# The relation loop's weights of a unit loaded by one transfer instead of six

## The chip, the cores and the metric

The kernel runs on one core of a Trainium2 chip. The metric is the device time of a whole execution in microseconds; of several runs the median is given.

## The reference

A graph with 625 nodes and 10,625 edges goes through four layers, each of which adds its output to the rows x [625, 768] after a layer norm and relu. Everything is float32. The first layer is the one at issue; for each of 34 relations r it takes the mean of the source rows over the edges of that relation at each target node, multiplies by the relation's 768 x 768 matrix, and adds all relations up:

```python
seg = edge_type * n + dst
agg = jax.ops.segment_sum(x[src], seg, num_segments=N_REL * n)
cnt = jax.ops.segment_sum(ones, seg, num_segments=N_REL * n)
mean = agg.reshape(N_REL, n, -1) / jnp.maximum(cnt, 1.0).reshape(N_REL, n, 1)
h1 = jnp.einsum('rni,rio->no', mean, W_rel) + x @ W_root + b_rgcn
```

The rest of the first layer is a graph convolution on h1; after it come two graph convolutions, three relational layers with 3 relations, and one more graph convolution.

## The kernel before

The program sorts the edges twice (by relation and source tile for the later layers, by relation alone for the first), plans the first layer's work, runs the relation loop `add_means` (L1415), and then the other layers.

The plan cuts the sorted edges into units. A unit has up to 3 x 128 edges of one relation and two or three tiles of 128 target slots. For each unit the loop does this:

- POOL gathers the 3 x 128 source rows by indirect DMA (`gather`, L1536) into e_raw, [128, 3, 768].
- SyncE loads the unit's list of targets (L1507) and the relation's weights (L1512) into w_raw, [128, 6, 768]: six chunks of 128 input features, each 384 KB. In `load(u)` chunk f waits until VectorE has split chunk f of the unit before, since w_raw has one buffer; every chunk has a semaphore `w_loaded[f]`.
- Products are made of two float32r parts. ScalarE casts each e tile and each weight chunk to a high part (`split_e` L1594, `split_w` L1598), VectorE subtracts it from the raw values for the low part (L1647, L1652). The parts w_hi, w_lo, e_hi, e_lo have one buffer each.
- TensorE first forms the unit's sums (L1718): rows of e times a 0/1 matrix `pick` that VectorE makes from the list (L1641), 36 matmuls. ScalarE and VectorE copy them out as g_hi and g_lo (L1614, L1670). Then come the products (L1732) of g with w, 36 matmuls for each target tile.
- ScalarE and VectorE scale the result into y (L1627, L1680), and POOL adds y to the sums in memory by an indirect DMA (`scatter`, L1548).

The order on each engine is written out by hand; all run a loop over the units. ScalarE and VectorE split chunk 5 of unit u inside the unit, right after the first bank of sums. During the products of unit u they split, for unit u+1, in the order w0, w1, e0, w2, e1, w3, e2, w4; ScalarE's w_f waits until the products have used chunk f of unit u (`w_used`). Then both scale y. TensorE's sums of u+1 wait for all e_lo of u+1. POOL in its turn u waits for e_ready of unit u, gathers for u+1, waits for the scatters of u-1 and issues the scatters of u when y is there. Transfers of SyncE are in one queue, those of POOL in another.

Of the kernel before, what the change touches and what calls it, by code (L numbers as in the profile page):

```python
# [55 lines left out]
def semaphores(nc, tag, ctx):  # L56


    made = []

    def clear():
        nc.clear_and_free_semaphores(made)
        nc.all_engine_barrier()

    ctx.callback(clear)

    def sem(name):
        made.append(nc.alloc_semaphore(f"{tag}_{name}"))
        return made[-1]

    return sem
# [1343 lines left out]
def add_means(nc, tag, units, w_rel, rows, sums, plan, src_index, slot_dst, row_index, row_inv, targets):  # L1415
# [8 lines left out]
    fc = width // 128  # L1424
    half = width // 2
    with ExitStack() as ctx:
        def sb(name, shape, dt):
            return ctx.enter_context(nc.sbuf_tensor(f"{tag}_{name}", shape, dt))

        sem = semaphores(nc, tag, ctx)  # L1430
# [9 lines left out]
        w_raw = sb("w_raw", [128, fc, width], F32)  # L1440
# [4 lines left out]
        ps_y = ctx.enter_context(nc.psum_tensor(f"{tag}_ps_y", [SLOT, UNIT, 2, BANK], F32))  # L1445

        list_loaded = sem("list_loaded")
        w_loaded = [sem(f"w_loaded{f}") for f in range(fc)]
        index_ready = sem("index_ready")
        gathered = [sem(f"gathered{j}") for j in range(UNIT)]  # L1450
        scattered = [sem(f"scattered{j}") for j in range(UNIT)]
# [4 lines left out]
        w_ready = sem("w_ready")  # L1456
# [8 lines left out]
        def count(eng):  # L1465

            return eng.value_load(plan[0:1, 3, 0:1], min_val=1, max_val=units - 1)

        def unit(u):
            return nc.s_assert_within(u, 0, units - 2, skip_runtime_bounds_check_because="units - 1 bounds their number")  # L1470

        def has_third(eng, u):
            return eng.value_load(plan[0:1, 1, bass.ds(u, 1)], min_val=0, max_val=1)

        def if_third(eng, third, body):

            with eng.If(third):
                body(3)
            with eng.Else():
                body(2)  # L1480

        def per_bank(tiles):

            return BANK // (tiles * SLOT)

        def sums_in_bank(i, tiles):

            per = per_bank(tiles)
            bank = ps_y[:, 2, i - 2, :] if is_spare(i) else ps_g[:, i % 2, :]
            return bank[:, 0:per * tiles * SLOT].rearrange("p (c s) -> p c s", c=per)  # L1490
# [9 lines left out]
        @block.sync  # L1500
        def _(sp):
            def load(u, first):
                kind = sp.value_load(plan[0:1, 0, bass.ds(u, 1)], min_val=0, max_val=w_rel.shape[0] - 1)
                if not first:

                    sp.wait_ge(picked, u)
                sp.dma_start(list_now[:], targets[bass.ds(u, 1), :].broadcast_to([SLOT, UNIT_COLS])).then_inc(list_loaded, 16)  # L1507
                for f in range(fc):
                    if not first:

                        sp.wait_ge(w_ready, fc * u - fc + f + 1)
                    sp.dma_start(w_raw[:, f, :], w_rel[bass.ds(kind, 1), f * 128:(f + 1) * 128, :].rearrange("a f o -> f (a o)"))\  # L1512
                        .then_inc(w_loaded[f], 16)

            load(0, True)
            end = count(sp)
            with sp.Fori(1, end + 1) as u:
                load(nc.s_assert_within(u, 1, units - 1, skip_runtime_bounds_check_because="as above"), False)

            sp.wait_ge(w_loaded[fc - 1], 16 * end + 16)  # L1520
            sp.sem_inc(waited, 1)

        @block.gpsimd
# [64 lines left out]
        @block.scalar  # L1588
        def _(act):
            nc.scalar.preload_act_table(ACT.Copy)  # L1590

            def split_e(u, j):
                act.wait_ge(gathered[j], 16 * u + 16)
                nc.scalar.copy(e_hi[:, j, :], e_raw[:, j, :]).then_inc(e_hi_ready, 1)  # L1594

            def split_w(u, f):
                act.wait_ge(w_loaded[f], 16 * u + 16)
                nc.scalar.copy(w_hi[:, f, :], w_raw[:, f, :]).then_inc(w_hi_ready, 1)  # L1598

            for j in range(UNIT):  # L1600
                split_e(0, j)
            for f in range(fc - 1):
                split_w(0, f)

            nc.scalar.nop().then_inc(y_ready, 2)
            with act.Fori(0, count(act)) as n:
                u = unit(n)
                third = has_third(act, u)

                def split_g(tiles):  # L1610
                    per = per_bank(tiles)
                    for f in range(0, fc, per):
                        act.wait_ge(g_summed, fc * u + f + per)
                        nc.scalar.copy(g_hi[:, f:f + per, 0:tiles * SLOT], sums_in_bank(f // per, tiles)).then_inc(g_hi_ready, per)  # L1614
                        if f == 0:

                            split_w(u, fc - 1)

                if_third(act, third, split_g)

                for f in range(fc):

                    act.wait_ge(w_used, fc * u + f + 1)
                    if f == fc - 1:

                        act.wait_ge(y_free, u + 1)
                        nc.scalar.activation(y[:, 1, :].rearrange("p (a o) -> p a o", a=2), ps_y[:, 1, :, 0:half], ACT.Copy,  # L1627
                                             scale=row_inv[:, bass.ds(UNIT * u + 1, 1)]).then_inc(y_ready, 1)
                    else:
                        split_w(u + 1, f)  # L1630
                    if 0 < f <= UNIT:
                        split_e(u + 1, f - 1)
# [107 lines left out]
def gnn_kernel(nc, d, out):  # L1740
# [11 lines left out]
    with ExitStack() as ctx:  # L1752
# [17 lines left out]
        with ExitStack() as part:  # L1770
            def sb(name, shape, dt):
                return part.enter_context(nc.sbuf_tensor(name, shape, dt))

            slot_src = sb("s0_slot_src", [SLOT, UNIT * units], F32)
            slot_dst = sb("s0_slot_dst", [SLOT, UNIT * units], F32)
            src_index = sb("s0_src_index", [SLOT, UNIT * units], I32)
            row_index = sb("s0_row_index", [SLOT, UNIT * units], I32)
            row_inv = sb("s0_row_inv", [SLOT, UNIT * units], F32)
            plan = sb("s0_plan", [1, 4, units], I32)
            with ExitStack() as early:  # L1780
                lots = early.enter_context(nc.sbuf_tensor("s0_lots", [EP, types0], F32))
                tile_of = early.enter_context(nc.sbuf_tensor("s0_tile_of", [EP, EC], F32))
                sort_edges(nc, "s0_sort", d["src"], d["dst"], d["edge_type_34"], types0, UNIT, slot_src, slot_dst,
                           lots=lots, tile_of=tile_of,
                           aside=lambda where, block, sem: root_rows(nc, where, block, sem, h, d["L0_gnn_b_rgcn"],
                                                                     d["L0_gnn_W_root"], ident, rows0, sums0[0:N, :]))
                plan_units(nc, "s0_plan", d["dst"], types0, tile_of, lots, slot_src, slot_dst, units, src_index,
                           row_index, row_inv, targets, plan, dinv)
            add_means(nc, "l0_means", units, d["L0_gnn_W_rel"], rows0, sums0, plan, src_index, slot_dst, row_index,
                      row_inv, targets)  # L1790
# [56 lines left out]
```

## Time and profile before

| | |
|---|---|
| median of 3 runs | 2092.66 us (2090.81 to 2101.08) |
| profiled execution, first to last instruction | 2085.4 us |
| TensorE matmul busy | 1726.6 us (83%) |
| VectorE busy | 1171.2 us (56%) |
| ScalarE busy | 592.7 us (28%) |
| POOL busy | 327.8 us (16%) |
| mean granted TensorE clock | 0.906 |
| DMA | 230.03 MB, mean 110 GB/s |

Of the profiled execution no other time than its span is given, so the runs' median stands beside the span. Busy shares are means over stages. The relation loop lies between about 365 and 1140 us of the span. Rows name a line of the kernel, the engine, the operation and output<-inputs; "waited for" rows say which engine's work ended an idle time. PE is TensorE, DVE VectorE, ACT ScalarE, SP SyncE; the suffix q is an engine's sequencer, which issues its transfers. The granted clock is a share of full speed.

### The profile page before, as it was taken

The page shows a single profiled execution, that of the slowest core. Times are in us where ns is not written, and L with a number is a line of the kernel's source. Part 1 is how long each engine was busy: PE and PEld are TensorE (multiplying, and loading weights), DVE is VectorE, ACT ScalarE, POOL GpSimd, SP SyncE. Part 2 cuts the span into 40 slices and gives each one's busy share as a digit, 9 for nine tenths or more (in the row PEclk, how much of TensorE's full clock was granted, in tenths as well). Part 3 has the DMA queues.
Part 4 walks back from the last instruction along what each step waited for, and adds up shares of the span by engine and source line. Part 5 has one row for each costly group of instructions (what it writes and reads, how often), then busy time and mean ns, then how long its engine had stood idle before and what let it go on. Part 6 is the DMA issues. An engine that isn't in the chain of part 4 may idle for free. (4 is left out here: it accounts for less than half of the span.)

```text
span 2085.4 us, 30218 instructions
## 1 busy us (share of the span) xinstructions
PE 1726.6 (83%) x10272; PEld 1655.3 (79%) x10273; DVE 1171.2 (56%) x1803; ACT 592.7 (28%) x782; POOL 327.8 (16%) x301
## 2 busy tenths in 40 slices
PE   2633954779889788889897599899998999999988
PEld 2532834779889788889896599799998999999988
DVE  8678697556566555565564464733554433444463
ACT  0112100444454443354443322211222211222221
POOL 1005010333434343323333000000000000000000
PEclk9675975899999999999998699899999999999999
DMA  1012100676877777678666311221222111122211
GB/s 62 4 43 87 39 1 2 209 230 196 219 216 200 226 209 200 170 230 226 194 199 157 109 37 58 66 54 65 77 65 60 57 52 45 52 72 65 60 46 53
DMA packets 84461, 230.03 MB, mean 110 GB/s; under 512 B 10326, under 2 KB 22617, under 8 KB 84410
## 3 DMA queue, kind: packets, MB, share of 16 engines
q1 hardware_dynamic: 65066, 158.14, 23.5%
q0 software_dynamic: 19344, 71.18, 14.6%
q8 instruction: 35, 0.57, 0.1%
q14 instruction: 16, 0.13, 0.0%
HBM read 190.01 MB, written 39.28 MB: 110 GB/s over the span
## 5 line engine op out<-in xcount | busy, mean ns | idle before, releaser
L1062 PE MATMUL layers_ps_o<-layers_w_hi,layers_g_hi 128*125 128x384 f32 (+1 forms) x1040 | 362.5, 349 | 4.1 <-DVE layers_w_lo L926 2.9
L1063 PE MATMUL layers_ps_o<-layers_w_lo,layers_g_hi 128*125 128x384 f32 (+1 forms) x1040 | 361.1, 347 | 0.0
L1064 PE MATMUL layers_ps_o<-layers_w_hi,layers_g_lo 128*125 128x384 f32 (+1 forms) x1040 | 360.4, 347 | 0.0
L1652 DVE TENSOR_TENSOR l_means_w_lo<-l_means_w_raw,l_means_w_hi 128x768 fp32r<-128x768 f32 x209 | 199.3, 955 | 97.3 <-ACT l_means_w_hi L1598 85.6
L1087 PE MATMUL layers_ps_g<-a,h_hi 125*128 125x316 f32 x840 | 197.2, 317 | 52.9 <-DVE h_lo L554 40.0
L1732 PE MATMUL l_means_ps_y<-l_means_w_hi,l_means_g_hi 128*128 128x384 f32 x912 | 231.5, 334 | 0.0
L1732 PE MATMUL l_means_ps_y<-l_means_w_hi,l_means_g_lo 128*128 128x384 f32 x912 | 231.5, 334 | 0.0
L1732 PE MATMUL l_means_ps_y<-l_means_w_lo,l_means_g_hi 128*128 128x384 f32 x912 | 231.4, 334 | 0.0
L1718 PE MATMUL l_means_ps_g<-l_means_pick,l_means_e_hi 128*128 128x256 f32 (+1 forms) x408 | 131.4, 342 | 102.3 <-DVE l_means_e_lo L1647 102.3
L1598 ACT CAST l_means_w_hi<-l_means_w_raw 128x768 fp32r<-128x768 f32 x209 | 173.7, 833 | 136.7 <-PE l_means_ps_y L1732 120.5
L1062 PEld LDWEIGHTS layers_ps_o<-layers_w_hi,layers_g_hi 128*125 128x125 f32 x1040 | 194.1, 187 | 13.9 <-DVE layers_g_lo L931 4.3
L1548 POOL DMA_INDIRECT sums<-l_means_y,l_means_row_now x76 | 142.2, 1871 | 398.7 <-DVE l_means_y L1680 374.3
L1064 PEld LDWEIGHTS layers_ps_o<-layers_w_hi,layers_g_lo 128*125 128x125 f32 x1040 | 194.0, 187 | 5.5
L1063 PEld LDWEIGHTS layers_ps_o<-layers_w_lo,layers_g_hi 128*125 128x125 f32 x1040 | 193.9, 186 | 5.3
L1087 PE MATMUL layers_ps_g<-a,h_lo 125*128 125x316 f32 x840 | 195.3, 315 | 0.0
L1087 PEld LDWEIGHTS layers_ps_g<-a,h_hi 125*128 125x128 f32 x840 | 144.2, 195 | 57.6 <-DVE h_lo L554 41.5
L1647 DVE TENSOR_TENSOR l_means_e_lo<-l_means_e_raw,l_means_e_hi 128x768 fp32r<-128x768 f32 x105 | 100.2, 955 | 150.9 <-ACT l_means_e_hi L1594 150.6
L1718 PEld LDWEIGHTS l_means_ps_g<-l_means_pick,l_means_e_hi 128*128 128x128 f32 x408 | 93.7, 230 | 110.6 <-issue 110.6
L942 DVE SCALAR_TENSOR_TENSOR h_rows<-layers_ps_o,h_rows 125x768 f32<-125x768 f32 (+1 forms) x45 | 45.1, 1002 | 237.9 <-PE layers_ps_o L1064 237.9
L1732 PEld LDWEIGHTS l_means_ps_y<-l_means_w_hi,l_means_g_lo 128*128 128x128 f32 x912 | 164.7, 188 | 0.0
L1732 PEld LDWEIGHTS l_means_ps_y<-l_means_w_lo,l_means_g_hi 128*128 128x128 f32 x912 | 164.6, 188 | 0.0
L1732 PEld LDWEIGHTS l_means_ps_y<-l_means_w_hi,l_means_g_hi 128*128 128x128 f32 x912 | 163.4, 188 | 0.0
(281 smaller groups left out, 2572.3 us busy)
## 6 DMA issues: line engine op xcount, KB each, us to landing
l_means_w_raw<-in_L_gnn_W_rel SPq DMA_DIRECT2D x210, 384.0 KB
layers_w_raw<-in_L_gnn_w_rel SPq DMA_DIRECT2D x39, 384.0 KB, 3.3
layers_w_raw<-in_L_gnn_w_rel SPq DMA_DIRECT2D x21, 448.0 KB, 3.7
layers_a_raw<-adj SPq DMA_DIRECT2D x9, 769.0 KB
layers_w_raw<-in_L_gnn_W SPq DMA_DIRECT2D x18, 384.0 KB, 5.2
l_means_list_now<-targets SPq DMA_DIRECT2D x35, 192.0 KB
layers_w_raw<-in_L_gnn_w_root SPq DMA_DIRECT2D x13, 384.0 KB, 3.6
layers_w_raw<-in_L_gnn_w_root SPq DMA_DIRECT2D x7, 448.0 KB, 4.1
```

The costliest lines, as they stand in the source:

```text
L942: v.scalar_tensor_tensor(to, ps, by, base, ALU.mult, ALU.add).then_inc(o_taken, 1)
L1062: t.matmul(out, g_hi[:, f, rows], w_hi[:, f, cols], start=(f == 0), stop=False)
L1063: t.matmul(out, g_hi[:, f, rows], w_lo[:, f, cols], start=False, stop=False)
L1064: mm = t.matmul(out, g_lo[:, f, rows], w_hi[:, f, cols], start=False, stop=(f == fc - 1))
L1087: mm = t.matmul(ps_g[:, buf, at:at + PART[p]], rows[:, k, f * 128:(f + 1) * 128], a[:, k, cols], start=(k == 0 and part == 0), stop=(k == ...
L1548: nc.gpsimd.indirect_dma_start(out=sums, in_=y[:, j, :], in_offset=None, compute_op=ALU.add, out_offset=bass.IndirectOffsetOnAxis(ap=row_n ...
L1598: nc.scalar.copy(w_hi[:, f, :], w_raw[:, f, :]).then_inc(w_hi_ready, 1)
L1647: v.tensor_tensor(e_lo[:, j, :], e_raw[:, j, :], e_hi[:, j, :].bitcast(F32), ALU.subtract)\
L1652: v.tensor_tensor(w_lo[:, f, :], w_raw[:, f, :], w_hi[:, f, :].bitcast(F32), ALU.subtract)\
L1718: mm = t.matmul(sums, e[:, j, f * 128:(f + 1) * 128], pick[:, j, 0:cols], start=(j == 0 and part == 0), stop=(j == UNIT - 1 and part == 1))
L1732: mm = t.matmul(ps_y[:, j, o, 0:half], g[:, f, at], w[:, f, o * half:(o + 1) * half], start=(f == 0 and g is g_hi and w is w_hi), stop=(f ...
```

## The change

In the relation loop, the six weight transfers of a unit and their six semaphores become one transfer and one semaphore. The transfer waits until all six chunks of the unit before are split (`w_ready` at 6u). ScalarE's split of any chunk waits for the whole transfer. The list's transfer before it, the order of the splits and all else are unchanged.

```diff
@@ -1445,7 +1445,7 @@
-        w_loaded = [sem(f"w_loaded{f}") for f in range(fc)]
+        w_loaded = sem("w_loaded")
@@ -1505,19 +1505,18 @@
-                for f in range(fc):
-                    if not first:
-
-                        sp.wait_ge(w_ready, fc * u - fc + f + 1)
-                    sp.dma_start(w_raw[:, f, :], w_rel[bass.ds(kind, 1), f * 128:(f + 1) * 128, :].rearrange("a f o -> f (a o)"))\
-                        .then_inc(w_loaded[f], 16)
+                if not first:
+
+                    sp.wait_ge(w_ready, fc * u)
+                sp.dma_start(w_raw[:], w_rel[bass.ds(kind, 1), :, :].rearrange("a (f p) o -> p (a f) o", p=128))\
+                    .then_inc(w_loaded, 16)
...
-            sp.wait_ge(w_loaded[fc - 1], 16 * end + 16)
+            sp.wait_ge(w_loaded, 16 * end + 16)
@@ -1594,7 +1593,7 @@
             def split_w(u, f):
-                act.wait_ge(w_loaded[f], 16 * u + 16)
+                act.wait_ge(w_loaded, 16 * u + 16)
                 nc.scalar.copy(w_hi[:, f, :], w_raw[:, f, :]).then_inc(w_hi_ready, 1)
```

## Rows read from the trace of the kernel before

**Rows 1.** Window of the loop: us, engines' busy, PEclk, DMA share, GB/s.
```profile
377.80:1136.60 758.80, 669.13 (x3960) 660.63 (x3960) 435.38 (x579) 338.40 (x470) 270.85 (x244) 0.94 0.74 206
```

**Rows 2.** The page's costliest groups, one kind of product.
```profile
L1732 PE MATMUL l_means_ps_y<-l_means_w_hi,l_means_g_hi 128*128 128x384 f32 x912 | 231.5, 334 | 0.0
```

**Rows 3.** Waits of TensorE in the whole profile: total us, times, longest.
```profile
PE l_means_ps_g L1718 <- DVE l_means_e_lo L1647: 102.3, 26, 17.7
```

**Rows 4.** Windows, summed, of the 19 two-tile units after a two-tile unit.
```profile
sum 382.20, PE 344.53 PEld 338.55 DVE 232.18 ACT 180.55 POOL 139.48; mean PE 18.13 PEld 17.82 DVE 12.22 ACT 9.50 POOL 7.34
```

**Rows 5.** Windows, summed, of six two-tile units after a three-tile unit.
```profile
sum 148.60, PE 101.77 PEld 99.86 DVE 74.66 ACT 62.18 POOL 59.49; mean PE 16.96 PEld 16.64 DVE 12.44 ACT 10.36 POOL 9.91
```

**Rows 6.** Windows of the six three-tile units after a two-tile unit, two of them.
```profile
639.60:664.60 25.00, 25.00 (x144) 25.00 (x145) 14.24 (x20) 10.69 (x16) 8.16 (x7) 1.00 0.68 191
...
821.00:848.80 27.80, 27.78 (x145) 27.79 (x146) 14.40 (x20) 10.00 (x15) 6.56 (x7) 0.90 0.63 177
```

**Rows 7.** Timeline of VectorE in one unit: start, us, instruction, idle before.
```profile
712.11 0.96 DVE L1652 TENSOR_TENSOR l_means_w_lo<-l_means_w_raw,l_means_w_hi 128x768 fp32r<-128x768 f32 x1
...
718.62 0.96 DVE L1652 TENSOR_TENSOR l_means_w_lo<-l_means_w_raw,l_means_w_hi 128x768 fp32r<-128x768 f32 x1 [1.03 <-ACT l_means_w_hi L1598]
724.56 0.96 DVE L1647 TENSOR_TENSOR l_means_e_lo<-l_means_e_raw,l_means_e_hi 128x768 fp32r<-128x768 f32 x1 [4.98 <-ACT l_means_e_hi L1594]
...
728.10 0.95 DVE L1647 TENSOR_TENSOR l_means_e_lo<-l_means_e_raw,l_means_e_hi 128x768 fp32r<-128x768 f32 x1
```

**Rows 8.** Timeline of ScalarE in the same unit.
```profile
723.69 0.84 ACT L1594 CAST l_means_e_hi<-l_means_e_raw 128x768 fp32r<-128x768 f32 x1 [5.11 <-DMA l_means_e_raw<-rows,l_means_src_now]
...
726.96 0.83 ACT L1594 CAST l_means_e_hi<-l_means_e_raw 128x768 fp32r<-128x768 f32 x1
```

**Rows 9.** Timeline of TensorE, the first matmul of the next unit.
```profile
729.18 0.38 PE L1718 MATMUL l_means_ps_g<-l_means_pick,l_means_e_hi 128*128 128x256 f32 x1 [3.14 <-DVE l_means_e_lo L1647]
```

**Rows 10.** Timeline of SyncE's issues, 705 to 735.
```profile
706.40 7.17 SPq L1512 DMA_DIRECT2D l_means_w_raw<-in_L_gnn_W_rel  x4
...
717.75 16.02 SPq L1512 DMA_DIRECT2D l_means_w_raw<-in_L_gnn_W_rel  x6
```

**Rows 11.** Waits of ScalarE before the weight casts.
```profile
ACT l_means_w_hi L1598 <- PE l_means_ps_y L1732: 120.5, 77, 2.7
```

**Rows 12.** Lines L1512 and L159: issues, ns min/median/max, first and last start.
```profile
L1512 SPq DMA_DIRECT2D l_means_w_raw<-in_L_gnn_W_rel x210: 332/333/567, 365.5 to 1118.8; - x105
...
L159 SPq DMA_DIRECT2D sums<-s_sort_spare x1: 443/443/443, 7.8 to 7.8; - x1
```

**Rows 13.** Waits of SyncE before the weight issues.
```profile
SPq L1512 <- DVE l_means_w_lo L1652: 505.5, 200, 11.7
```

**Rows 14.** Timeline of VectorE ahead of the sums at 539.53.
```profile
534.97 0.96 DVE L1647 TENSOR_TENSOR l_means_e_lo<-l_means_e_raw,l_means_e_hi 128x768 fp32r<-128x768 f32 x1 [9.68 <-ACT l_means_e_hi L1594]
...
539.32 0.95 DVE L1652 TENSOR_TENSOR l_means_w_lo<-l_means_w_raw,l_means_w_hi 128x768 fp32r<-128x768 f32 x1
```

**Rows 15.** Timeline of TensorE, the sums at 539.53.
```profile
539.53 0.57 PE L1718 MATMUL l_means_ps_g<-l_means_pick,l_means_e_hi 128*128 128x256 f32 x1 [7.78 <-DVE l_means_e_lo L1647]
```

**Rows 16.** Windows for the DMA engines (last two columns: share, GB/s).
```profile
713.00:727.00 14.00, 13.04 (x77) 12.72 (x75) 6.70 (x11) 5.35 (x8) 5.83 (x7) 1.00 0.88 239
...
375.00:377.00 2.00, 0.00 (x0) 0.00 (x0) 1.28 (x2) 1.29 (x3) 0.00 (x0) 0.50 1.00 389
```

**Rows 17.** Timeline of POOL, the first gather of the unit at 709.
```profile
716.23 1.04 POOL L1536 DMA_INDIRECT l_means_e_raw<-rows,l_means_src_now  x1 [0.84 <-POOL l_means_src_now L1533]
```

**Rows 18.** The page's DMA issues, a later layer's weights: KB each, us to landing.
```profile
layers_w_raw<-in_L_gnn_w_rel SPq DMA_DIRECT2D x39, 384.0 KB, 3.3
```

**Rows 19.** Windows of the sums of two units, granted clock third from the end.
```profile
539.50:545.70 6.20, 6.17 (x37) 6.17 (x38) 3.82 (x5) 1.91 (x3) 3.21 (x2) 0.67 0.67 159
...
559.10:563.40 4.30, 4.30 (x36) 4.30 (x37) 3.50 (x5) 2.21 (x4) 1.63 (x1) 1.00 0.63 183
```

## The prediction

> **What bounds the kernel now.** I read the loop first, then its units, then one unit engine by engine. The relation loop takes 758.8 us of the profiled execution [rows 1]. It has 34 units: the 912 matmuls of each product kind are 76 tiles of 12, so 26 units of two tiles and 8 of three [rows 2] (in the windows below, 108 or 144 matmuls). TensorE's longest waits in the whole profile stand there, 26 of them, all for e_lo, the last input that a unit's sums need [rows 3]. So the loop is not bound by TensorE in two-tile units. The order of units, read off the starts of the sums, gives classes: 19 two-tile units after a two-tile one, 20.1 us each with 18.1 busy [rows 4]; 7 two-tile units after a three-tile one, 24.8 us each in the six that are followed by another, with 17.0 busy [rows 5]; 6 three-tile units after a two-tile one, busy throughout, 25.0 or 25.1 us and, once, 27.8 [rows 6]; and two more three-tile units, the first and the last but one.
>
> One unit in detail, its sums starting at 709.0; I call that S. VectorE splits the unit's own last chunk (w5) at S+3.1 to S+4.1, makes the pick, then splits w0 and w1 of the next unit, w1 at S+9.6, and stands idle 4.98 us until the first gathered tile is there [rows 7]. ScalarE's own wait in front is for the gather [rows 8]. From S+15.6 six passes e0, w2, e1, w3, e2, w4 follow each other, e2 ends at S+20.1, and the next sums start at S+20.2 [rows 7, 9]. The point for this change is that no weight is waited for: SyncE sends each chunk as soon as its old content is split [rows 10], so chunks 0 to 4 of the next unit are sent up to a whole unit ahead, and only w5 is sent within the unit itself. ScalarE's waits before w_hi are for the products that free w_hi, 120.5 us in 77 waits, and none is for a weight transfer [rows 11].
>
> **What the change removes.** Five issues per unit on SyncE, 0.33 us each [rows 12]. SyncE is no bound: it waits for VectorE 505.5 us at that line [rows 13]. Gain taken: nothing. Its cover is that wait, and if it were gone, 5 x 0.33 = 1.7 us a unit would be the most. A single three-piece transfer from 128 partitions took 0.44 us to issue [rows 12], so the new issue is priced at 0.4 us. The loop's list transfer is still sent ahead of the weights and waits for the same pick: no change, and the pick is made before the next list is needed.
>
> **What it adds: a wait.** The one transfer may start only when all six chunks of the unit before are split, that is after its w5, S+4.1. And the first split of the next unit needs all six to have landed. Transfer and splitting, which went on side by side, now stand one behind the other. The sequence is w5 split, transfer T, then w0, w1, e0, w2, e1, w3, e2 on VectorE, then the sums.
>
> *The tail behind the landing.* In the unit before 539.53 the passes from e0 to w4 ran without a gap at 0.87 us each, from 534.97, and the sums started 4.56 us after e0 started [rows 14, 15]. Two more passes (w0, w1) make 4.56 + 2 x 0.87 = 6.3, and ScalarE's cast ahead of the first makes 0.9 [rows 8]: the next sums start 7.2 us after the landing. Behind the waiting cast ScalarE also has the casts of e, so an e that is there earlier does not help.
>
> *The transfer.* It is 6 x 128 x 3 KiB = 2.36 MB. From 713 to 727 the DMA engines moved 239 GB/s x 14 us = 3.35 MB at a share of 0.88 [rows 16]. That is just the unit's traffic: two scattered tiles 0.79, three gathered 1.18, the list 0.20, and three weight chunks (w5, w0, w1) 1.18. The other three chunks went in the quieter end. Now all six are asked for in this stretch: 1.18 MB more. With weights nearly alone the engines did 389 GB/s at share 1.00 [rows 16], so 3.0 us more. Against that stands the unused 12% of 14 us, 1.7 us, which a waiting transfer can fill. The stretch ends at 728.3 to 730.0, S+19.3 to S+21.0; the gather shares the engines from S+7.2 [rows 17] and the weights finish last but for the list behind them (0.5 us). Landing: S+18.8 to S+20.5. I take S+19.3, near the lower end, because a queue that always has weight packets fills the gaps. Lower bound of all: a 384 KB chunk in the later layers lands in 3.3 us [rows 18], of which 1.0 is its data at 389 GB/s, so the six on idle engines would land 2.3 + 6.1 = 8.4 us after the issue, S+12.9.
>
> *The clock.* TensorE would idle from about S+17 to S+26.5. After an idle of 7.8 us the next sums ran at a mean granted clock of 0.67 and took 6.2 us, where at clock 1.00 they took 4.3 [rows 15, 19]; the levels are 1.2 and 2.4 GHz. This puts the w5 split at S+5.3 instead of S+4.1; scatter occupies the engines then in any case, and S+19.3 has that start in it.
>
> **The sum.** Two-tile after two-tile: period 19.3 + 7.2 = 26.5 against 20.1, +6.4, times 19 = 122 us. Two-tile after three-tile: three scatters keep the gather late already, so the weights (sent at S+4.0, first sums fast) land by about S+18 and the tail would end at S+25.2; what binds is still the gather, delayed by the extra weight traffic, between 0 and 3.0 us. I take 1.5, times 7 = 10 us. Three-tile units: products cover the transfer (S+19.3 + 7.2 is before 27.8), but their sums now come after an idle TensorE, as in the one of 27.8 us: +2.7 for five of the six [rows 6], 13 us. First unit: its products wait until all six chunks have landed, 1 us. Sum +146 us. The profiled execution is given by its span, 2085.4, which becomes 2231; the median of the three runs shown, 2092.66, stands 7.3 above it, so 2239 us.
>
> **A page against this.** The trace has no large weight transfer to time. The Trainium skill, DMA: Bandwidth & Descriptors, Rules for kernel authors, wants at least 1 MiB per DMA on 128 partitions, and its section Anatomy of one DMA gives about 2.0 us plus bytes / 436 GB/s (for the gpsimd path); an estimate from it is 7.4 us for this one. The same table also says to issue early and wait late, which is what is lost here. By its formula alone the landing would be at S+12.7, the rival next.
>
> **Rivals.**
> A. *The weights get through first.* For it: with 2.36 MB asked for at once they may take more than their share, and the idle-engine bound is S+12.9. The gather then ends 3.0 us later than now (its last cast starts at S+18.0 [rows 8]), at S+20.9, and with the 2.2 us from there to the next sums the period is 23.1: +3.0 x 19, +3.0 x 7, +13 = 91 us, 2184. Against it: scatter and gather are queued over the same stretch, which is already at 0.88. This is also where the formula of the Trainium skill's DMA page leads.
> B. *The clock stays up,* as in the unit at 559.1. Then w5 is split 1.2 us earlier, the landing is about S+18, the period 25.2, three-tile units stay at 25.1: 19 x 5.1 + 10 = 107, 2200.
> C. *Weights starve.* Scatter and gather hold the engines, landing at S+21.3, 28.5 a period: 19 x 8.4 + 7 x 3.5 + 14 = 198, 2291.
> D. *Hidden, no change:* needs landing by S+12.9 and a gather no later. Excluded by the share 0.88 unless the scatter's share is mostly idle waiting.
> E. *Faster.* Place: the gather. If the burst is over before the gather's first packet, w0 and w1 (0.79 MB, 2.0 us) no longer share the engines with it, and the period falls from 20.1 to 18.1: 19 x 2 = -38, 2055. It decides only if the burst lands by S+10, under 6 us after its issue, less than its data take at 389 GB/s.
>
> **Chances.** Forecast 0.65, A 0.10, B 0.12, C 0.08, D 0.03, E 0.02. The range runs from A to just short of C, 2180 to 2285; it holds the bounds of the landing (S+18.8 and S+20.5 are 19 x -0.5 and 19 x +1.2, so 2229 and 2262) and B. A measurement here tells about 0.5%, 10 us, from no change. Faster 0.02, same 0.03, slower 0.95.
>
> **What would show it.** One weight issue a unit, about S+4 to S+5.4, and none within the products. ScalarE's first w_hi of the next unit waits for the weight transfer, and then seven casts follow without a gap. TensorE's waits for e_lo stay about 26 in number but grow to 8 to 10 us each. Two-tile units of 25 to 28 us with granted clock under 1.00 at the sums, three-tile units of 27.8. The stages before 365 and after 1150 unchanged. I am wrong if the landing is before S+15, if the seven casts still wait for the gather, or if two-tile periods stay near 20.

## The result and the profile after

The changed kernel takes 2261.19 us (median of 4 runs, 2259.78 to 2264.04) against 2091.73 of the kernel before in the same series: a ratio of 1.079 [1.077, 1.082], 169.5 us slower. Forecast were 2239 us, +146, with a range of 2180 to 2285. The profiled execution took 2264.04 us as a whole and 2262.0 from first to last instruction, so only 2 us lie around the span. The spans differ by 176.6 us, 7 more than the medians: before's profiled execution lay some 4 us below its median, and the changed kernel's is the longest of its four, 2.9 us above.

The windows of the units, grouped as in [rows 4 to 6]: the 19 two-tile units after a two-tile one, the six after a three-tile one, and the six three-tile units (columns as there: TensorE, its weight loads, VectorE, ScalarE, POOL).

```profile
sum 537.60, PE 363.27 PEld 357.29 DVE 228.21 ACT 175.78 POOL 136.81; mean PE 19.12 PEld 18.80 DVE 12.01 ACT 9.25 POOL 7.20
...
sum 153.30, PE 102.24 PEld 100.35 DVE 76.34 ACT 60.70 POOL 55.08; mean PE 17.04 PEld 16.72 DVE 12.72 ACT 10.12 POOL 9.18
...
sum 164.70, PE 163.52 PEld 162.72 DVE 80.38 ACT 58.39 POOL 39.63; mean PE 27.25 PEld 27.12 DVE 13.40 ACT 9.73 POOL 6.61
```

| units | before, us | forecast | after | share of the loss |
|---|---|---|---|---|
| 19 two-tile after two-tile | 20.1 | 26.5 | 28.3 | 19 x 8.2 = 155.4 |
| 7 two-tile after three-tile | 24.8 | 26.3 | 25.6 (six) | 7 x 0.8 = 5.5 |
| 6 three-tile after two-tile | 25.5 | 27.7 | 27.5 | 6 x 1.9 = 11.5 |

The three, taken from the unrounded sums, make 172 of the spans' 176.6 us. In the first class VectorE and ScalarE do what they did; what grew is idle time. Waits in the loop of the changed kernel, most time first, others left out at the dots:

```profile
ACT l_means_w_hi L1597 <- DMA l_means_w_raw<-in_L_gnn_W_rel: 428.6, 34, 15.1
DVE l_means_w_lo L1651 <- ACT l_means_w_hi L1597: 409.5, 41, 14.2
...
PE l_means_ps_g L1717 <- DVE l_means_e_lo L1646: 245.4, 28, 18.8
...
ACT l_means_w_hi L1597 <- PE l_means_ps_y L1731: 12.0, 1, 12.0
ACT l_means_e_hi L1593 <- DMA l_means_e_raw<-rows,l_means_src_now: 11.6, 8, 8.1
```

Before, ScalarE waited for no weights at all, only for the products that free w_hi [rows 11]; that wait has all but gone, and 34 waits for the weights stand in its place. The wait for the gather, 156 us in the loop before, is down to 11.6: the gathered tiles are there, but their casts stand behind one that waits. TensorE's wait went from 102 us in 26 [rows 3] to 245 in 28.

One two-tile unit whose sums start at S = 623.0. First ScalarE, then VectorE, SyncE and TensorE (start, us, instruction, idle before and what ended it):

```profile
629.91 0.59 ACT L1613 CAST l_means_g_hi<-l_means_ps_y 128x512 fp32r<-128x512 f32 x1 [0.85 <-PE l_means_ps_y L1717]
643.91 1.56 ACT L1597 CAST l_means_w_hi<-l_means_w_raw 128x768 fp32r<-128x768 f32 x2 [13.41 <-DMA l_means_w_raw<-in_L_gnn_W_rel]
645.38 0.83 ACT L1593 CAST l_means_e_hi<-l_means_e_raw 128x768 fp32r<-128x768 f32 x1
...
648.31 0.83 ACT L1593 CAST l_means_e_hi<-l_means_e_raw 128x768 fp32r<-128x768 f32 x1
```
```profile
627.41 0.96 DVE L1651 TENSOR_TENSOR l_means_w_lo<-l_means_w_raw,l_means_w_hi 128x768 fp32r<-128x768 f32 x1
...
644.77 1.83 DVE L1651 TENSOR_TENSOR l_means_w_lo<-l_means_w_raw,l_means_w_hi 128x768 fp32r<-128x768 f32 x2 [12.37 <-ACT l_means_w_hi L1597]
...
649.99 0.95 DVE L1646 TENSOR_TENSOR l_means_e_lo<-l_means_e_raw,l_means_e_hi 128x768 fp32r<-128x768 f32 x1
```
```profile
628.54 0.38 SPq L1511 DMA_DIRECT2D l_means_w_raw<-in_L_gnn_W_rel  x1
```
```profile
651.07 0.58 PE L1717 MATMUL l_means_ps_g<-l_means_pick,l_means_e_hi 128*128 128x256 f32 x1 [8.77 <-DVE l_means_e_lo L1646]
```

w5 is split by S+5.4, the transfer goes out at S+5.5 (0.38 us to issue), the first cast starts at S+20.9, seven casts follow without a gap, the last e part is ready at S+27.9 and the sums start at S+28.1. From the cast to the sums are 7.16 us; 7.2 was forecast. TensorE idles 8.77 us before the next sums. This unit's own sums, which came after such an idle too, ran at a granted clock of 0.61 and took 6.6 us:

```profile
623.00:629.60 6.60, 6.55 (x36) 6.56 (x37) 3.76 (x5) 1.90 (x3) 3.59 (x3) 0.61 0.28 30
```

### The profile page after: what moved, and what is told of

Same layout as the page of the kernel before. It is cut to its first block and busy times, and to the rows that moved or that the text cites. A ratio compares the mean times of both kernels' runs of the same rounds, so it can differ in the third digit from the quotient of the medians.

```text
span 2262.0 us, 29557 instructions
## 1 busy us (share of the span) xinstructions
PE 1756.1 (78%) x10272; PEld 1683.5 (74%) x10273; DVE 1162.0 (51%) x1803; ACT 581.1 (26%) x782; POOL 310.9 (14%) x301
## 5 line engine op out<-in xcount | busy, mean ns | idle before, releaser
L1717 PE MATMUL l_means_ps_g<-l_means_pick,l_means_e_hi 128*128 128x256 f32 (+1 forms) x408 | 154.2, 389 | 245.4 <-DVE l_means_e_lo L1646 245.4
L1717 PEld LDWEIGHTS l_means_ps_g<-l_means_pick,l_means_e_hi 128*128 128x128 f32 x408 | 110.6, 271 | 255.0 <-issue 254.5
L1062 PEld LDWEIGHTS layers_ps_o<-layers_w_hi,layers_g_hi 128*125 128x125 f32 x1040 | 194.2, 187 | 14.8 <-issue 5.0
L1547 POOL DMA_INDIRECT sums<-l_means_y,l_means_row_now x76 | 137.1, 1804 | 483.0 <-DVE l_means_y L1679 455.2
L864 ACT CAST layers_w_hi<-layers_w_raw 128x768 fp32r<-128x768 f32 (+1 forms) x104 | 89.7, 863 | 251.5 <-PE layers_ps_o L1064 243.2
```

The lines of the kernel that those rows point to most:

```text
L864: nc.scalar.copy(w_hi[:, f, :], w_raw[:, f % ring, :]).then_inc(w_hi_ready, 1)
L1062: t.matmul(out, g_hi[:, f, rows], w_hi[:, f, cols], start=(f == 0), stop=False)
L1547: nc.gpsimd.indirect_dma_start(out=sums, in_=y[:, j, :], in_offset=None, compute_op=ALU.add, out_offset=bass.IndirectOffsetOnAxis(ap=row_n ...
L1717: mm = t.matmul(sums, e[:, j, f * 128:(f + 1) * 128], pick[:, j, 0:cols], start=(j == 0 and part == 0), stop=(j == UNIT - 1 and part == 1))
```

## The experiments

### The two waits apart: e1, e2, e6

The change does two things at once: it sends all weights late, and it lets no split begin before all have landed. e1 does the first alone and e2 the second alone, both with six small transfers; e6 does both, still with six.

e1, late start:

```diff
                 for f in range(fc):
-                    if not first:
+                    if not first and f == 0:
-                        sp.wait_ge(w_ready, fc * u - fc + f + 1)
+                        sp.wait_ge(w_ready, fc * u)
```

> The kernel before, but all six weight transfers of a unit wait for the last split of the unit before, as the changed kernel's one transfer does; each keeps its own semaphore, so the first chunk can be split when it has landed. My theory (the loss is made by the late start and the common landing together, since only together do they put the transfer and the splitting one behind the other): w0 lands by about S+9 and is split among the products, the gather is as late as in the changed kernel (S+19.7), the next sums start 2.2 us after it: two-tile units of about 22 us, 2092 + 19 x 1.9 + 7 x 0.8 = about 2135 us. Rival (the late start alone is the loss): two-tile units near 28 us, about 2260 us. For the size of the transfer: if one large transfer lands later than six small ones, w5 lands clearly before S+21 here.

Measured 2135.03 us, ratio 1.018 [1.015, 1.021]; two-tile units 411.6 / 19 = 21.7 us. Time and period are as expected, the way there only in part: in the unit with S = 593.0 w0 is cast at S+13.0 and not about S+9, and ScalarE waits there for w0, w1 and w2 and not for the gather. Over the loop it waits 139.1 us for weights and 114.2 for the gather.

e2, one semaphore:

```diff
-        w_loaded = [sem(f"w_loaded{f}") for f in range(fc)]
+        w_loaded = sem("w_loaded")
...
-                act.wait_ge(w_loaded[f], 16 * u + 16)
+                act.wait_ge(w_loaded, 16 * fc * u + 16 * fc)
```

> The kernel before with its six transfers at their own times, but one semaphore for all: no split of a unit before all six chunks have landed. My theory: w5 is sent at S+4 and lands by S+9, so w0's split slips from S+7.6 to about S+10, still ahead of the gather at S+15: no change, 2092 us within 10. Rival (the common semaphore alone is the loss): TensorE's waits grow, near 2260 us.

Measured 2079.29 us, ratio 0.993 [0.991, 0.995]: no loss, and 14 us gained, a little more than the 10 that were allowed. The gather lands a median of 6.5 us after its issue here and 7.3 in the kernel before; no run shows how much of the gain that makes.

e6 has both edits.

> Both halves of the change's timing with the six small transfers kept: all six sent after the last split, none of the splits before all have landed (one semaphore). My theory (the two waits together are the whole loss, and the size of the transfer has no part): 2261 us within 10, landing about S+20 to S+21. Rival (the large transfer itself lands later): clearly less, 2240 or lower.

Measured 2277.54 us, ratio 1.088 [1.085, 1.091]. ScalarE's waits for the weights in the kernels e1, e2 and e6, in this order:

```profile
ACT l_means_w_hi L1598 <- DMA l_means_w_raw<-in_L_gnn_W_rel: 139.1, 62, 6.3
```
```profile
ACT l_means_w_hi L1598 <- DMA l_means_w_raw<-in_L_gnn_W_rel: 105.0, 28, 6.1
```
```profile
ACT l_means_w_hi L1598 <- DMA l_means_w_raw<-in_L_gnn_W_rel: 449.6, 35, 16.4
```

The late start alone costs 42 us, the common wait alone gives 14, the two together cost 183 (each against the kernel before in its own series). The loss is not the sum of the parts. Late chunks that are split one by one as they land still overlap with their transfer; a common landing of chunks that left a unit ahead is early enough. Only both put transfer and splits one behind the other. That was the forecast's mechanism, and the rivals, each part as the whole cause, are out. For e6 the 2261 us were missed all the same.

The size of the transfer has a part too, which I had expected to be within 10 us: with the same waits one large transfer is 16 us quicker than six small ones. It is all in one class: two-tile units after a three-tile one take 171.8 / 6 = 28.6 us in e6 and 25.6 in the changed kernel, while those after a two-tile one take 526.3 / 19 = 27.7 against 28.3.

The traces show what makes the first class. Its sums ran at full clock, so the weights are asked for at S+4.3, before the scatters' packets come. The large transfer is issued in 0.38 us, the six take 3.2 us to issue. Queues and packets of the 6 us after the issue (q1 is SyncE's queue, q0 POOL's), in the changed kernel (S = 542.2, from 546.2) and in e6 (S = 545.5, from 549.5); then the issue and the first cast in each:

```profile
q1 hardware_dynamic: 432, 1.33, 69.5%
q0 software_dynamic: 27, 0.08, 7.7%
```
```profile
q1 hardware_dynamic: 330, 0.92, 49.5%
q0 software_dynamic: 55, 0.17, 29.2%
```
```profile
546.46 0.38 SPq L1511 DMA_DIRECT2D l_means_w_raw<-in_L_gnn_W_rel  x1
560.19 1.56 ACT L1597 CAST l_means_w_hi<-l_means_w_raw 128x768 fp32r<-128x768 f32 x2 [12.73 <-DMA l_means_w_raw<-in_L_gnn_W_rel]
```
```profile
549.76 3.18 SPq L1512 DMA_DIRECT2D l_means_w_raw<-in_L_gnn_W_rel  x6
567.19 1.56 ACT L1598 CAST l_means_w_hi<-l_means_w_raw 128x768 fp32r<-128x768 f32 x2 [16.44 <-DMA l_means_w_raw<-in_L_gnn_W_rel]
```

The large transfer has 0.41 MB more through before the scatters fill the engines. At the 0.145 MB/us that the weights get beside a scatter (next section) that is an estimate of 2.8 us, and the first cast comes at S+18.0 instead of S+21.7. In the other class the weights are asked for at S+5.5, behind the scatters, in both kernels; why the six are there 0.6 us sooner is open.

### What holds the transfer up: e7, e8

The same edit in both:

```diff
-                if_third(pool, third, add)
+                del add
...
-                for j in range(2):
-                    pool.wait_ge(scattered[j], 16 * u + 16)
...
                 pool.sem_inc(waited, 1)
-                with pool.If(third):
-                    pool.wait_ge(scattered[2], 16 * thirds)
-                    pool.sem_inc(waited, 1)
```

The changed kernel without scatters:

> The changed kernel without the scatters (the sums are not added to memory), so the weights share the engines with the gather alone. My theory (the landing is late because scatter and gather hold the engines): landing by S+13 to S+15, two-tile units 20.5 to 22 us, about 2095 us. Rival (one large transfer lands late by itself, whoever shares the engines): landing at S+18 or later, over 2190 us.

The kernel before without scatters:

> The kernel before without the scatters. My theory: the gather is there in time, TensorE binds, two-tile units of 16.8 to 17.5 us wherever they stand, about 1970 us, so the change costs some 120 us even without scatters, for want of an overlap of transfer and splits. Rival (without the scatters the transfer is hidden behind the products, and both kernels are the same): a difference under 20 us.

One run each: 2159.81 and 1970.91 us. In e7 two-tile units take 457.3 / 19 = 24.1 us; in one with S = 477.8 the first cast starts at S+17.2:

```profile
494.96 1.57 ACT L1592 CAST l_means_w_hi<-l_means_w_raw 128x768 fp32r<-128x768 f32 x2 [10.64 <-DMA l_means_w_raw<-in_L_gnn_W_rel]
```

That is 3.7 us earlier than with scatters, so they hold the transfer up, but S+13 to S+15 was too early: it is hardly later than the S+12.9 of idle engines, and the gather shares the engines here. The transfer's 2.36 MB and the gather's 1.18 at 389 GB/s with the 2.3 us of [rows 18] make 11.4 us from the issue at S+5.5, an estimate of S+16.9. Neither expectation of e7 fits as written; the measured landing lies between them, and the total nearer to the rival's, though a transfer that gains 3.7 us is not one that is late by itself. e8 came out as expected in its time and its units, but not in the difference: the change costs 189 us without scatters and not 120, more than with them, since the kernel before gains 121 us and the changed one 101.

The queues' packets in the changed kernel (queue, packets, MB, share of the 16 engines), from 627 to 644, the unit's whole traffic; then from 634 to 636, when scatter and weights are under way, and from 638 to 640, when gather and weights are:

```profile
DMA packets 1456, 4.52 MB, mean 266 GB/s; under 512 B 112, under 2 KB 240, under 8 KB 1456
q0 software_dynamic: 528, 1.97, 46.1%
q1 hardware_dynamic: 928, 2.56, 41.4%
```
```profile
q0 software_dynamic: 92, 0.28, 70.8%
q1 hardware_dynamic: 93, 0.29, 38.9%
```
```profile
q0 software_dynamic: 101, 0.51, 61.3%
q1 hardware_dynamic: 105, 0.32, 39.7%
```

Where both queues have work they get packet for packet, 92 against 93, but a scatter's packet takes 0.708 x 2 x 16 / 92 = 0.25 us of an engine and a weight's 0.389 x 32 / 93 = 0.13. (The shares add up to more than 100%, since packets overlap.) So the weights get about one third of the engines' time while a scatter runs, 0.145 MB/us instead of 0.389. Beside the gather it is the same, 101 against 105 packets and 0.16 MB/us, but there the other queue moves 0.51 MB in the 2 us and not 0.28. The Trainium skill, DMA: Bandwidth & Descriptors, Queues, rings and completion order, says that each engine takes turns between its queues by packets; the equal counts agree.

### The clock: e3

```diff
+FILL = 60
...
                         mm.then_inc(w_used, 1)
+                    if tiles == 2:
+                        for i in range(FILL):
+                            t.matmul(ps_g[:, 0, 0:2 * SLOT], g_hi[:, 0, 0:SLOT], g_hi[:, 0, 0:2 * SLOT], start=True, stop=True)
```

> The changed kernel with 60 further matmuls (256 columns, into a bank of sums that nobody reads any more) after the products of each two-tile unit, 7 us of work in an idle of about 9 us. My theory: the granted clock of the sums is 1.00, they take 4.3 us instead of 5.7 to 7.0, w5 is split 1.2 us earlier and the weights are sent 1.2 us earlier, but into a stretch where the scatter holds the engines, so the landing moves by 0.5 to 1.2 us: two-tile units of 26.7 to 27.4 us instead of 27.9, three-tile units 1 us shorter, 2261 - 10 to -30, so 2230 to 2250 us. Rival (the clock has no part): 2261 us, or more if the matmuls are in the way.

Measured 2229.76 us, ratio to before 1.065 [1.062, 1.068], 31 us under the changed kernel. Two-tile units take 508.8 / 19 = 26.8 us. In one with S = 621.5, the sums, the issue and the first cast:

```profile
621.50:626.00 4.50, 4.47 (x37) 4.48 (x38) 3.69 (x5) 1.91 (x3) 1.63 (x1) 1.00 0.00 0
```
```profile
625.78 0.38 SPq L1512 DMA_DIRECT2D l_means_w_raw<-in_L_gnn_W_rel  x1
641.02 1.57 ACT L1598 CAST l_means_w_hi<-l_means_w_raw 128x768 fp32r<-128x768 f32 x2 [14.24 <-DMA l_means_w_raw<-in_L_gnn_W_rel]
```

The weights are asked for at S+4.3 and not S+5.5, and the first cast starts at S+19.5 and not S+20.9: the landing moves by all of the earlier issue, where 0.5 to 1.2 us was expected. The fall of the clock after TensorE's idle (granted clock 0.61 in the unit above, 1.00 here) is thus a real part of the loss, some 31 of 169 us, and rival B has its place and its sign; it does not hold in the changed kernel itself.

### The order of the splits: e9

On both engines e0, e1, e2, then y, then w0 to w4; here VectorE's part; ScalarE's is alike, with its waits for the products ahead of e0 and of y:

```diff
+                for j in range(UNIT):
+                    split_e(u + 1, j)
+                if_third(dve, third, take_y)
                 for f in range(fc - 1):
                     split_w(u + 1, f)
-                    if 0 < f <= UNIT:
-                        split_e(u + 1, f - 1)
-                if_third(dve, third, take_y)
```

> The changed kernel with the splits in another order on ScalarE and VectorE: e0, e1, e2, then y, then w0 to w4, so that the gathered tiles are not queued behind the casts that wait for the weights. My theory (the tail of 7.2 us from the landing to the next sums is made by seven casts in the one order; of the cycle then only transfer, six weight splits and the w5 split are left, since the buffer forces these one behind the other): two-tile units of 21.5 to 23.5 us instead of 28.3, about 2150 us, between 2135 and 2175. Rival (the landing alone sets the period, whatever the order): within 20 us of 2261.

Measured 2120.27 us (2108.08 to 2133.61), ratio 1.014 [1.008, 1.021]: 141 us of the loss gone, with the single transfer and its late start kept. VectorE in one unit:

```profile
578.30 0.96 DVE L1643 TENSOR_TENSOR l_means_e_lo<-l_means_e_raw,l_means_e_hi 128x768 fp32r<-128x768 f32 x1 [6.91 <-ACT l_means_e_hi L1593]
...
583.65 4.43 DVE L1648 TENSOR_TENSOR l_means_w_lo<-l_means_w_raw,l_means_w_hi 128x768 fp32r<-128x768 f32 x5
```

The waits are again for the gather, as before the change; ScalarE's come to 351.1 us in 101 times. The two-tile units take 386.7 / 19 = 20.4 us. The time is below my 2135: I had summed transfer and splits to a cycle with the transfer at its full length, but the five weight splits ran without a wait behind y, so the weights were there and the gather bound the unit.

### Other groupings: e4, e10, e5

All three keep a wait and a semaphore for each group; only the groups differ. e4 has `groups = ((0, 5), (5, 6))`.

```diff
-                for f in range(fc):
-                    if not first:
-                        sp.wait_ge(w_ready, fc * u - fc + f + 1)
-                    sp.dma_start(w_raw[:, f, :], w_rel[bass.ds(kind, 1), f * 128:(f + 1) * 128, :].rearrange("a f o -> f (a o)"))\
-                        .then_inc(w_loaded[f], 16)
+                for g, (a, b) in enumerate(groups):
+                    if not first:
+                        sp.wait_ge(w_ready, fc * u - fc + b)
+                    sp.dma_start(w_raw[:, a:b, :], w_rel[bass.ds(kind, 1), a * 128:b * 128, :]
+                                 .rearrange("a (f p) o -> p (a f) o", p=128)).then_inc(w_loaded[g], 16)
```

e4, groups of 5 and 1:

> Two transfers and two semaphores: chunks 0 to 4 in one (1.97 MB), sent when the fifth chunk is split at the end of the unit before, and w5 in one of its own at its own time. My theory: chunks 0 to 4 land by about S+9, before the gather, so nothing of the loss is left; w0 and w1 no longer share the engines with the gather, which may come up to 1 us earlier: 2065 to 2095 us. Rival (a large transfer in place of several costs by itself): clearly over 2095 us, towards 2260.

Measured 2080.92 us, ratio 0.993 [0.991, 0.996]. As expected: a transfer of 1.97 MB costs nothing when it leaves before w5.

e10, groups of 3 and 3:

> Two transfers, chunks 0 to 2 when the third is split and chunks 3 to 5 when w5 is split (S+4). My theory (a chunk sent late costs nothing if its split comes late in the order: w3 is wanted at S+17 and these three land by about S+14): no loss, 2060 to 2095 us. Rival (any group that waits for w5 puts its transfer in the path): over 2120 us.

Measured 2102.37 us, ratio 1.005 [1.003, 1.007]: outside what I expected, though far from the rival. Two-tile units take 400.2 / 19 = 21.1 us. ScalarE's largest waits in the loop are not for the weights:

```profile
ACT l_means_e_hi L1595 <- DMA l_means_e_raw<-rows,l_means_src_now: 161.5, 35, 8.6
ACT l_means_w_hi L1599 <- PE l_means_ps_y L1733: 137.7, 87, 2.7
```

The three late chunks are in time. In e10 a gather lands a median of 7.4 us after its issue, in e4 6.9, so the late chunks seem to hold it up; but in the kernel before it is 7.3, so this does not explain the unit's 1.0 us over before. Half of that is TensorE's busy time (18.6 us a unit against 18.1); the rest is open.

e5, groups of 3, 2 and 1:

> Three transfers with three semaphores: chunks 0 to 2 sent when the third chunk is split (S+17, when the gather has landed and the engines are free), chunks 3 and 4 at the end of the unit's splits, w5 at its own time. My theory from the two runs that came out faster than before (weights out of the gather's way give the gather back up to 2.0 us, the 0.79 MB of w0 and w1 at 389 GB/s): two-tile units 18.1 to 19.5 us instead of 20.1, those after a three-tile unit 22.3 instead of 24.8; 2093 - 12 to -38 - 17, so 2040 to 2065 us. Rival (the gather is not held up by the weights; the two faster runs are for another reason, fewer issues or semaphores): 2080 us like them.

Measured 2062.64 us, ratio 0.985 [0.983, 0.987]. The windows of the 19 and of the six two-tile units, and the gather's landing (min, median, max):

```profile
sum 367.90, PE 339.41 PEld 334.58 DVE 231.63 ACT 179.31 POOL 140.75; mean PE 17.86 PEld 17.61 DVE 12.19 ACT 9.44 POOL 7.41
...
sum 134.20, PE 101.73 PEld 99.81 DVE 74.54 ACT 62.17 POOL 59.48; mean PE 16.96 PEld 16.64 DVE 12.42 ACT 10.36 POOL 9.91
```
```profile
DMA to landing us min/median/max: 4.5/5.7/8.7
```

19.4 and 22.4 us a unit against 20.1 and 24.8. The gather lands 5.7 us after its issue, against 7.3 in the kernel before. The same bytes, most of them sent when scatter and gather do not want the engines, beat both kernels: 31 us under the one before, 199 under the changed one.

## Why the prediction was right, and what was off

**Bound before.** The gather bound the two-tile units: e8, in which the scatters ahead of it are gone (which also lets POOL issue it at S+5.2 instead of S+7.2), brings them from 20.1 to 325.1 / 19 = 17.1 us with 16.9 busy, and e5 gains by freeing the gather.

**What is removed.** Nothing was gained over the kernel before from fewer issues, as forecast. Once the start is late, though, the issues are in the path, and one is 16 us better than six (e6). The new issue took 0.38 us, 0.4 was taken.

**The added wait.** Right, and shown from both sides: neither half of it costs much alone (e1, e2), both cost 183 us (e6).

**The tail.** 7.2 us forecast, 7.16 measured. That it is the order of the casts that puts e0 to e2 behind the landing is shown by e9.

**The transfer.** This is the term that was mis-sized. Landing was put at S+19.3 with an upper bound of S+20.5; 28.3 - 7.2 makes it S+21.1 in the mean. The bytes were right (4.52 MB between 627 and 644), and so was the engines' work: 0.88 x 14 + 3.0 = 15.3 us forecast, 0.87 x 17 = 14.8 measured. The gaps were filled too, as I had assumed. Most of the 1.7 us unused before lay in the last 2 us of the stretch, and in the changed kernel there is none between 633 and 641 (before, then after; the share is the last number but one):

```profile
725.00:727.00 2.00, 1.04 (x6) 0.72 (x5) 2.00 (x3) 1.78 (x4) 0.00 (x0) 1.00 0.46 183
...
633.00:641.00 8.00, 8.00 (x48) 8.00 (x47) 0.00 (x0) 0.00 (x0) 1.39 (x3) 1.00 1.03 360
```

What failed is the sentence under the clock, that S+19.3 "has that start in it". The stretch was read from a unit whose sums ran at clock 1.00 and whose w5 was split at S+4.1; in the changed kernel it is S+5.4. I let the scatter cover that delay, and e3 shows that it does not: with the clock back the first cast is at S+19.5 in the unit shown and at 26.8 - 7.2 = S+19.6 in the mean, which is the landing that I forecast. So of the 1.8 us that the landing came later, 1.5 are the slow start, 19 x 1.5 = 29 of 34 us. The landing also lies above the S+20.5 that I gave as its upper bound. That the total still came out just under the 2262 us of that bound is luck: the other classes lost less than forecast, and the 7.3 us added for the median stood for before's profiled execution alone. Span against span the forecast is 31 us short (2231 against 2262.0), median against median 22.

**The classes.** Two-tile units after a three-tile one lost 0.8 us and not 1.5, three-tile units 1.9 as the clock's price said (+2.2 in the mean of six was forecast). These take 6 us off; with the 34 the sum of 146 comes to 174, near the 176.6 of the spans.

**The clock.** The sums took 6.6 us in the unit shown where 6.2 was taken. The price of the slow clock by itself is 31 us (e3); rival B put it at 39. The forecast had it for the three-tile units and at nothing for the landing, which is where most of it fell.

**Rivals.** A needed the weights to get through first; the counts of packets speak against it, and where the weights do get ahead, after a three-tile unit, they land at S+18.0. C's landing and period, S+21.3 and 28.5, are nearer to the measured S+21.1 and 28.3 than my own, and scatter and gather do hold the engines; its total was too high because of its other terms. D and E are out; but E's mechanism, the weights' 0.79 MB out of the gather's way, is real: e5 built it on purpose and got 0.8 of the 2.0 us in one class and 2.4 in the other.

**The formula.** By what the Trainium skill, DMA: Bandwidth & Descriptors, Anatomy of one DMA, gives for one large DMA the landing would have been S+12.7, 8.4 us too early: it knows of no other traffic. Its advice to issue early and wait late (Rules for kernel authors) fits e4 and e5, where larger transfers that left early cost nothing.

## What to carry to other kernels

Before six transfers are merged into one, ask when the last of the buffers comes free and when the first of the chunks is read: a merged transfer can start only when the last buffer is free and must have landed when the first chunk is read. If the chunks are read one by one and have one buffer, the overlap of transfer and reading is gone. Merge those whose buffers come free together, and choose the moment by who else wants the DMA engines; here three groups at good times gave 1.5% where one group cost 7.9%. In a queue of casts in fixed order, put what arrives early ahead of what arrives late.

## What the runs showed of the hardware that was not expected

A queue of 3 KiB copies beside an accumulating scatter got as many packets but one third of the engines' time (93 and 92 packets, 38.9% and 70.8%). One transfer of 2304 KB was 16 us quicker over the kernel than six of 384 KB with the same waits, in units where it was asked for just ahead of the scatters: it had 1.33 MB through in 6 us, the six 0.92. And a late transfer costs twice: the idle that it makes on TensorE lowered the granted clock of the next sums to 0.61, which sent the next transfer 1.2 us later (S+5.5 instead of S+4.3) and made it land 1.4 us later, 31 us in all.
